# Two expert layers: the product back to the features in three rounded products

## What is computed

```python
x = _layernorm(x + _L0_attn_ref(x, Wqkv, Wout))          # causal attention, 16 heads of 8
x = _layernorm(x + _L0_ffn_ref(x, Wg, W1, W2, W3))       # 8 experts of 256, 2 per token
x = _layernorm(x + _L1_attn_ref(x, w_qkv, w_out, b_out)) # rotary positions, 16 heads of 8
x = _layernorm(x + _L1_ffn_ref(x, ...))                  # 4 experts of 512, 2 per token
```

## Time and profile before

| | |
|---|---|
| median of 3 runs | 2009.62 us (2008.22 to 2015.79) |
| the profiled execution | 2016.69 us, its span 2014.8 us |
| TensorE busy | 1766.9 us, 88% |
| VectorE | 1391.3 us, 69% |
| ScalarE | 1165.4 us, 58% |
| GpSimd | 96.9 us, 5% |
| first expert stage, first product back to last | 485.2 to 881.4 us |
| second expert stage, the same | 1696.7 to 2004.2 us |

### The profile page before, as it was taken

The page is one execution under the profiler, slowest core; times in us unless marked ns, Lnnn a source line. Parts: engine busy times, 40 slices in busy tenths (PEclk is TensorE's granted clock), DMA queues, the critical chain, the costliest instruction groups (busy, mean ns, idle before and its releaser), DMA issues.

```text
span 2014.8 us, 31350 instructions
## 1 busy us (share of the span) xinstructions
PE 1766.9 (88%) x9328; PEld 853.9 (42%) x9328; DVE 1391.3 (69%) x2540; ACT 1165.4 (58%) x1801; POOL 96.9 (5%) x123
## 2 busy tenths in 40 slices
PE   4558888886999999976999999999999986999897
PEld 2223333334655666632333333333333324554454
DVE  2257777775677777747788888898898834455544
ACT  2347777773444444420777777777777773444443
POOL 1000000000111001111000000000000000001100
PEclk8679999997999999985999999999999996999999
DMA  4441111101011010112000000010000001000000
GB/s 153 142 120 48 48 45 46 50 29 63 0 32 32 31 32 31 32 37 64 21 22 21 20 20 21 23 36 21 21 20 20 21 1 42 6 6 5 10 5 11
DMA packets 43323, 71.06 MB, mean 35 GB/s; under 512 B 13408, under 2 KB 22512, under 8 KB 42624
## 3 DMA queue, kind: packets, MB, share of 16 engines
q1 hardware_dynamic: 43264, 70.37, 10.8%
HBM read 44.14 MB, written 26.21 MB: 35 GB/s over the span
## 4 chain that ended last, share of the span: by engine, by line
PE 63%; DVE 9%; ACT 8%; DMA 7%; SPq 6%; issue 5%; POOL 1%; DVEq 0%; ACTq 0%; POOLq 0%
PE full_o L687 13%; PE score L674 11%; PE hid_pair L957 11%; PE bank L1057 9%; ACT probs L736 6%; DMA q_st<-q_scr 4%; PE max_pair L650 3%; PE causal_o L451 3%; SPq L614 2%; PE triple L435 2%; SPq L615 2%; PE bank L966 2%; DMA xs<-in_x 2%; PE bank L987 2%; DVE hid L1314 1%
## 5 line engine op out<-in xcount | busy, mean ns | idle before, releaser
L774 DVE TENSOR_REDUCE negmax<-max_pair 128x1 f32<-128x1024 f32 x512 | 599.9, 1218 | 69.4 <-PE max_pair L650 62.2
L736 ACT ACTIVATE probs<-score 128x512 f32<-128x512 f32 x1024 | 529.1, 604 | 150.7 <-PE score L674 150.7
L650 PE MATMUL max_pair<-k_st,q_st 64*128 64x512 f32 x1024 | 405.5, 474 | 22.4 <-DMA q_st<-q_scr 18.2
L674 PE MATMUL score<-q_st,k_st 64*128 64x512 f32 x1024 | 383.1, 451 | 33.4 <-ACT probs L736 24.4
L484 ACT ACTIVATE cprobs<-triple 128x1536 f32<-128x1536 f32 x192 | 271.3, 1451 | 95.9 <-PE triple L435 95.6
L674 PEld LDWEIGHTS score<-q_st,k_st 64*128 64x128 f32 x1024 | 170.7, 185 | 304.3 <-ACT probs L736 283.0
L687 PE MATMUL full_o<-probs,v_st 128*32 128x512 f32 x2048 | 273.1, 606 | 0.0
L650 PEld LDWEIGHTS max_pair<-k_st,q_st 64*128 64x128 f32 x1024 | 171.7, 191 | 80.3 <-DVE negmax L774 39.6
L957 PE MATMUL hid_pair<-x_hi,w_hi 128*128 128x512 f32 x384 | 205.6, 535 | 0.0
L435 PE MATMUL triple<-q_st,k_st 64*128 64x512 f32 (+3 forms) x768 | 146.8, 415 | 43.4 <-DMA q_st<-q_scr 36.8
L451 PE MATMUL causal_o<-cprobs,v_st 128*32 128x512 f32 (+3 forms) x1536 | 161.4, 517 | 21.2 <-DVE cprobs L514 17.6
(11 more groups left out here) (127 smaller groups left out, 1612.0 us busy)
## 6 DMA issues: line engine op xcount, KB each, us to landing
k_st<-k_scr SPq DMA_DIRECT2D x128, 64.0 KB
q_st<-q_scr SPq DMA_DIRECT2D x128, 64.0 KB
q_st<-q_scr SPq DMA_DIRECT2D x16, 512.0 KB
k_st<-k_scr SPq DMA_DIRECT2D x64, 104.0 KB
q_scr<-qk_hi SPq DMA_DIRECT2D x24, 256.0 KB, 2.9
k_scr<-qk_hi SPq DMA_DIRECT2D x24, 256.0 KB, 3.0
q_scr<-qk_lo SPq DMA_DIRECT2D x16, 256.0 KB, 2.9
k_scr<-qk_lo SPq DMA_DIRECT2D x16, 256.0 KB, 3.1
```

The source lines that it names most:

```text
L650: ins = nc.tensor.matmul(ring[slot][:, half, :], q_st[p][rows, qt * P:(qt + 1) * P], k_st[p][rows, j, half * CH:(half + 1) * CH], start=Tr ...
L674: nc.tensor.matmul(sbank[L.score_bank(e)][:, :], k_st[p][rows, j, kt * P:(kt + 1) * P], q_st[p][rows, q0:q0 + w], start=True, stop=True, t ...
L736: nc.scalar.activation(probs[s % NP][:, j, :], sbank[L.score_bank(e)][:, :], ACT.Exp, scale=SCALE).then_inc(L.exp_done, 1)
L774: nc.vector.tensor_reduce(negmax[:, qt // TPC, j, qt % TPC:qt % TPC + 1], ring[slot][:, :, :].rearrange("p a n -> p (a n)"), AXX, ALU.max, ...
```

## The change

The product back becomes three rounded products. Its weight (`w3`, `we2`) is split once a stage: `w2_hi` by ScalarE, the lower half by VectorE. Each block `hid` is split too: `hid_hi` by a rounding copy on ScalarE, one step behind the activation, `hid_lo` = `hid` - `hid_hi` by a subtraction on GpSimd. The product back waits for the lower half. `hid`, `hid_hi` and `hid_lo` have four buffers (`HB` = 4). The first products run three blocks ahead in both stages; in the first stage step 0 issues two of them and step 15 none. The banks (`h_banks`) stay as they are. GpSimd's work beside is now placed by step, behind the subtraction of its step. `we2` is loaded into the second weight's tile, and the four `rot` tiles share memory with halves of q and k.

```diff
@@ experts' tiles @@
-            hid = [osb(f"hid{i}", [P, CH]) for i in range(2)]
+            hid = [osb(f"hid{i}", [P, CH]) for i in range(HB)]
+            hid_hi = [osb(f"hid_hi{i}", [P, CH], F32R) for i in range(HB)]
+            hid_lo = [osb(f"hid_lo{i}", [P, CH], F32R) for i in range(HB)]
...
-        h_banks, h_lead = [2, 4], [1, 2]
+        h_banks, h_lead = [2, 4], [3, 3]
...
@@ pe_chunk @@
-                lead = n + h_lead[layer]
-                if lead < SPC:
-                    pe_hidden(pe, st, c, par, lead, layer)
-                elif front is not None:
-                    pe_hidden(pe, st, front, 1 - par, lead - SPC, layer)
+                for lead in pe_leads(n, layer):
+                    if lead < SPC:
+                        pe_hidden(pe, st, c, par, lead, layer)
+                    elif front is not None:
+                        pe_hidden(pe, st, front, 1 - par, lead - SPC, layer)
...
-                pe.wait_ge(st.hid_ready, c * SPC + n + 1)
-                nc.tensor.matmul(bank[0][:, :], w[:, n, :], hid[n % 2][:, :], start=(layer == 0 and n == 0),
-                                 stop=(n == SPC - 1)).then_inc(st.y_done, 1)
+                pe.wait_ge(st.hid_lower, c * SPC + n + 1)
+                w_up, w_low = w2_hi[:, n, :], (w3_lo if layer == 0 else we2_lo)[:, n, :]
+                for a, (w, x) in enumerate(((w_up, hid_hi), (w_low, hid_hi), (w_up, hid_lo))):
+                    last = nc.tensor.matmul(bank[0][:, :], w, x[n % HB][:, :],
+                                            start=(layer == 0 and n == 0 and a == 0), stop=(n == SPC - 1 and a == 2))
+                last.then_inc(st.y_done, 1)
+
+        def pe_leads(n, layer):
+
+            k = h_lead[layer]
+            if layer == 1:
+                return [n + k]
+            if n == SPC - 1:
+                return []
+            return [n + k] if n else [n + k - 1, n + k]
...
@@ act_chunk @@
+        def act_upper(act, st, c, n):
+
+            act.wait_ge(st.hid_ready, c * SPC + n + 1)
+            wait_used(act, st.y_done, c * SPC + n - HB + 1)
+            nc.scalar.activation(hid_hi[n % HB][:, :], hid[n % HB][:, :], ACT.Copy).then_inc(st.hid_upper, 1)
...
+                if n > 0:
+                    act_upper(act, st, c, n - 1)
                 act_beside(act, st, n, back, front, 1 - par, layer)
...
+            act_upper(act, st, c, SPC - 1)
             act.wait_ge(st.y_done, (c + 1) * SPC)
...
@@ act_end and dve_end, once a stage @@
+                    w2 = w3_raw if layer == 0 else we2_raw
+                    nc.scalar.activation(w2_hi[:, :, :], w2[:, :, :], ACT.Copy).then_inc(w2_upper, 1)
...
+                if n == plan[layer].norm + 1:
+                    dve.wait_ge(w2_upper, layer + 1)
+                    w2, low = (w3_raw, w3_lo) if layer == 0 else (we2_raw, we2_lo)
+                    nc.vector.tensor_tensor(low[:, :, :], w2[:, :, :],
+                                            w2_hi[:, :, :].bitcast(F32), ALU.subtract).then_inc(w2_lower, 1)
...
@@ dve_chunk @@
-                wait_used(dve, st.y_done, c * SPC + n - 1)
+                wait_used(dve, st.hid_lower, c * SPC + n - HB + 1)
...
@@ GpSimd @@
+        def pool_lower(pool, st, c, n):
+
+            pool.wait_ge(st.hid_upper, c * SPC + n + 1)
+            wait_used(pool, st.y_done, c * SPC + n - HB + 1)
+            nc.gpsimd.tensor_tensor(hid_lo[n % HB][:, :], hid[n % HB][:, :], hid_hi[n % HB][:, :].bitcast(F32),
+                                    ALU.subtract).then_inc(st.hid_lower, 1)
...
+            if back is not None:
+                if n == pl.norm2 - 1 - (layer == 0):
+                    bc.at(back)
+                    pool_rstd(pool, bc, st.stats2, st.rstd2, 1, back + 1)
+                for a, at in enumerate((pl.q, pl.k)):
+                    if n == at:
+                        pool.wait_ge(st.rot_done, 2 * back + a + 1)
+                        nc.gpsimd.tensor_tensor(rot[2 * a][:, :], rot[2 * a][:, :], rot[2 * a + 1][:, :],
+                                                ALU.add).then_inc(st.rot_sum, 1)
+            if front is not None and n == pl.norm - 1:
+                fc.at(front)
+                pool_rstd(pool, fc, st.stats, st.rstd, 0, front + 1)
...
+            for n in range(SPC):
+                pool_lower(pool, st, c, n)
+                pool_beside(pool, st, n, back, front, layer)
```

More of the change, by code:

```diff
@@ L38 @@
 CP = 6
+HB = 4
 PAIRS = KT * HG
@@ L280, in build_program @@
         with ExitStack() as overlay:
-            w_raw = [osb(f"w_raw{k}", [P, NH * P]) for k in range(2)]
+            with ExitStack() as raw_only:
+                w_raw = [raw_only.enter_context(nc.sbuf_tensor(f"w_raw{k}", [P, NH * P], F32)) for k in range(2)]
+            w_lo = [osb(f"w_lo{k}", [P, NH * P], F32R) for k in range(2)]
             w_hi = [osb(f"w_hi{k}", [P, NH * P], F32R) for k in range(2)]
-            w_lo = [osb(f"w_lo{k}", [P, NH * P], F32R) for k in range(2)]
+            we2_raw, we2_lo = (w[1][:, :].rearrange("p (n c) -> p n c", c=P) for w in (w_raw, w_lo))
+            w2_hi = osb("w2_hi", [P, NH, P], F32R)
             x_out = osb("x_out", [P, TPC, D])
@@ L301, in build_program @@
             qk_lo = [osb(f"qk_lo{i}", [P, CH]) for i in range(4)]
+            rot = [qk_hi[2], qk_hi[3], qk_lo[2], qk_lo[3]]
             expert_raw = osb("expert_raw", [2 * E0, E0, P])
@@ L955, in pe_hidden @@
             for k in range(2 if layer == 0 else 1):
-                for a, (w, x) in enumerate(((w_hi[k], x_hi[par]), (w_lo[k], x_hi[par]), (w_hi[k], x_lo[par]))):
-                    last = nc.tensor.matmul(hbank[2 * k + n % h_banks[layer]], w[:, slice_of(n)], x[:, :], start=(a == 0),
+                w_up, w_low = w_hi[k][:, slice_of(n)], w_lo[k][:, slice_of(n)]
+                for a, (w, x) in enumerate(((w_up, x_hi[par]), (w_low, x_hi[par]), (w_up, x_lo[par]))):
+                    last = nc.tensor.matmul(hbank[2 * k + n % h_banks[layer]], w, x[:, :], start=(a == 0),
                                             stop=(a == 2))
@@ L1040, in pe_chunk @@
             per = SPC // n_exp[layer]
-            w = w3 if layer == 0 else we2
             for n in range(SPC):
@@ L1065, in pe_end @@
             pe.wait_ge(w_lower, 2 if layer == 0 else 3)
-            if layer == 1:
-                pe.wait_ge(we2_loaded, 16)
-            for n in range(h_lead[layer]):
+            pe.wait_ge(w2_lower, layer + 1)
+            for n in range(h_lead[layer] - (layer == 0)):
                 pe_hidden(pe, st, 0, 0, n, layer)
@@ L1309, in dve_chunk @@
                     dve.wait_ge(st.s_done, h_banks[layer] + c * SPC + n + 1)
-                    nc.vector.tensor_tensor(hid[n % 2][:, :], act_s[n % 2][:, :], lin_u[n % 2][:, :],
+                    nc.vector.tensor_tensor(hid[n % HB][:, :], act_s[n % 2][:, :], lin_u[n % 2][:, :],
                                             ALU.mult).then_inc(st.hid_ready, 1)
@@ L1346, in pool_rstd @@
             nc.gpsimd.tensor_tensor(rstd[:, k, :], rstd[:, k, :], mhalf[:, :], ALU.pow).then_inc(sig, 1)
-        def pool_back(pool, pc, st, c, layer):
-            pool_rstd(pool, pc, st.stats2, st.rstd2, 1, c + 1)
-            if layer == 0:
-                for a in range(2):
-                    pool.wait_ge(st.rot_done, 2 * c + a + 1)
-                    nc.gpsimd.tensor_tensor(rot[2 * a][:, :], rot[2 * a][:, :], rot[2 * a + 1][:, :],
-                                            ALU.add).then_inc(st.rot_sum, 1)
@@ L1356, in pool_end @@
-        def pool_end(pool, st, layer):
-            pc = Chain(pool, st.pool_chain)
-            for c in range(2):
-                pool_rstd(pool, pc, st.stats, st.rstd, 0, c + 1)
-            with pool.Fori(0, 2 * B - 2) as c:
-                pc.at(2 + 2 * c)
-                pool_back(pool, pc, st, c, layer)
-                pool_rstd(pool, pc, st.stats, st.rstd, 0, c + 3)
-            for c in (2 * B - 2, 2 * B - 1):
-                pc.at(2 + 2 * (2 * B - 2) + c - (2 * B - 2))
-                pool_back(pool, pc, st, c, layer)
+        def pool_lower(pool, st, c, n):
[3 more added lines that the diff above has]
+                                    ALU.subtract).then_inc(st.hid_lower, 1)
@@ new lines, in build_program, with pool_chunk @@
+        pool_front, pool_back = [None], [None]
+        def pool_chunk(pool, st, c, back, front, layer):
+            for n in range(SPC):
+                pool_lower(pool, st, c, n)
+                pool_beside(pool, st, n, back, front, layer)
+        def pool_end(pool, st, layer):
+            pool_front[0], pool_back[0] = Chain(pool, st.pool_chain), Chain(pool, st.pool_back_chain)
+            for n in range(SPC):
+                pool_beside(pool, st, n, None, 0, layer)
+            pool_chunk(pool, st, 0, None, 1, layer)
+            with pool.Fori(1, 2 * B - 1) as c:
+                pool_chunk(pool, st, c, c - 1, c + 1, layer)
+            pool_chunk(pool, st, 2 * B - 1, 2 * B - 2, None, layer)
```

(2 more changed lines are left out.)

26 lines of the change are left out of this document (18 added, 8 removed).

## The result

The changed kernel takes 2556.9 us (median of 4 runs, 2551.0 to 2560.2) against 2011.5: a ratio of 1.270, 95% interval 1.268 to 1.273, or 545 us more. The forecast was 2370, its range 2200 to 2470. The direction was right and the size was not.

A forecast was written before the change was run, and what follows sets the result against it. It took waits on same-step products, through ScalarE's order and the first stage's two banks, to bind: 2016.7 + 217 (first stage) + 140 (second) + 5 (weight splits) = 2379 us profiled, so 2370; range 2200 to 2470.

The forecast's parts named there:

- rival (d): Both expert stages: GpSimd binds by rate; at 31 us a chunk it is under both stages, no chance of its own.
- The first loop, ScalarE's order: Both stages: the product back waits on ScalarE work that needs products of the same step; a gate-row step 4.35 us.
- The second loop, two banks at a lead of three: First stage: block n+3 starts only after activation and `lin_u` of n+1 free a bank; steps up to 6.4 us.
- Rival (b): First stage: without the bank loop, near 63 us a chunk, 2230 in all; 20% together with other partial overlap.
- The steps of the first stage: Sixteen step times listed for a first-stage chunk, sum 80.6 us against 51.2 before; +217 us for the stage.
- The steps of the second stage: Sixteen step times listed for a second-stage chunk, sum 59.2 us against 40.4 before; +140 us for the stage.
- the clock stays near 1: TensorE in both stages: listed as a sign that the forecast is right; waits of 1.75 us leave it at 1.00.
- Rival (a): TensorE's granted clock falls for part of a stage; a third at half clock gives 2550, a tenth 2420; 12%.
- the upper bound: GpSimd's subtraction takes 1.96 us if it always waits for a `hid`, instead of 1.27; 100 us more.
- Products: Product back on TensorE: three rounded products take 0.70 us instead of 0.86 a block, 41 us less work.
- Both weights' split: Before each stage: a copy and a subtraction of 2048 columns for the product back's weight, +5 us for both.
- The subtraction's lower bound: The subtraction takes 0.68 us, as the same form does on VectorE, instead of 1.27; 85 us less.

The follow-up runs named there:

- e4: Changed kernel with ScalarE's upper half of block n moved ahead of the gate copy of n; 2430 us, ratio 1.209.
- e9: Changed kernel with first products one and two blocks ahead as before the change, and the product back done one block later; 2168 us, ratio 1.078.
- e3: Changed kernel with first products one and two blocks ahead as before the change, nothing left out; 2785 us, ratio 1.386.
- e2: Changed kernel without the halves of `hid`: all three products back read a rounded `hid`, first products three blocks ahead; 2241 us, ratio 1.114.
- e7: Changed kernel with first products two blocks ahead in the first stage, three in the second as before; 2392 us, ratio 1.189.
- e12: Changed kernel with first products done three times in nine second-stage steps that have a wait; 2510 us, ratio 1.248.
- e1: Changed kernel without the halves of `hid`: three products back read a rounded `hid`, first products one and two blocks ahead; 1987 us, ratio 0.989.
- e6: Changed kernel with the subtraction for the lower half on VectorE, behind `hid` of the next block; 2516 us, ratio 1.250.

## Why the prediction was right in kind and short in size

**Which resource binds.** Right. Neither ScalarE (51% busy) nor GpSimd (17%) is short of time; the new links cost as latency. GpSimd has no rate problem: rival (d) is out.

**The first loop, ScalarE's order.** Right. In the second stage nothing else holds TensorE for long. With the upper half moved ahead (e4) 127 us come off, and with the product back a step later at the same lead (e9 against e3) the chunk falls from 70.3 to 49.8.

**The second loop, two banks at a lead of three.** Right, and shown by e2 (+254 us with no halves at all) and e7. Rival (b), that only one loop binds, is out in the first stage.

**The steps of the first stage.** One middle chunk, steps 0 to 15 by the starts of the product back (the next ones repeat it within 0.15 us a step): 7.6, 5.7, 4.4, 5.9, 5.2, 6.6, 8.5, 8.2, 6.1, 6.4, 4.4, 6.7, 8.4, 3.0, 4.4, 4.0. Steps 1, 2, 9, 10, 14 and 15 have the clock at 1.00 and are within 0.25 us of the forecast; 4 and 5, at 0.93, are 0.2 and 0.5 over. Step 3 is 3.1 over: the normalisation above holds `lin_u`, and then its six first products run at half clock (763.22 to 765.92), which is 6 x 0.20 = 1.2 of the 3.1. Steps 0, 6, 7, 8, 11 and 12 have the clock between 0.50 and 0.77 and are together 11.5 over. Step 13, at 0.75, is 0.7 under, which hides as much of the miss. Steps 0, 6, 10 and 12 and the end of step 3 in the sums by stretch, of the kernel after (the clock is the third number from the end):

```profile
742.28:749.85 7.57, 7.08 (x17) 4.83 (x18) 1.98 (x3) 3.77 (x7) 2.37 (x2) 0.55 0.00 0
...
763.22:765.92 2.70, 2.70 (x6) 2.12 (x7) 1.18 (x2) 0.00 (x0) 0.00 (x0) 0.50 0.00 0
...
777.77:786.24 8.47, 6.82 (x16) 4.12 (x14) 2.58 (x4) 1.60 (x3) 2.57 (x2) 0.70 0.00 0
...
807.05:811.45 4.40, 2.94 (x12) 1.61 (x10) 1.76 (x4) 1.60 (x3) 1.34 (x1) 1.00 0.00 0
...
818.13:826.53 8.40, 6.41 (x20) 5.06 (x18) 4.68 (x22) 4.59 (x7) 1.27 (x1) 0.50 0.00 0
```

Step 0 is the plainest: it has 12 first products, each 0.43 instead of 0.23 apart at half clock, which is 12 x 0.20 = 2.4 us, and it is 2.5 over.

**The steps of the second stage.** Here the same step can be read at two clocks. In steps 1, 3, 7 and 9 TensorE has no wait to speak of. In the kernel after (chunk from 2215.67) they last 3.58, 2.73, 2.73 and 2.73 us at a clock of 0.50, in e12 (chunk from 2200.31) 1.94, 1.70, 1.49 and 1.70 at 1.00, step 7 at 0.92; the forecast had 1.9, 1.4, 1.4 and 1.4. Steps 1 and 9 of both, after first:

```profile
2221.48:2225.06 3.58, 3.58 (x11) 2.89 (x11) 1.01 (x3) 0.00 (x0) 1.18 (x1) 0.50 0.00 0
2255.51:2258.24 2.73, 2.73 (x6) 2.17 (x7) 0.50 (x1) 0.00 (x0) 1.63 (x1) 0.50 0.00 0
```

```profile
2205.43:2207.37 1.94, 1.94 (x11) 1.63 (x11) 0.50 (x1) 0.00 (x0) 1.19 (x1) 1.00 0.00 0
2234.53:2236.23 1.70, 1.65 (x7) 1.05 (x7) 0.49 (x1) 0.00 (x0) 1.64 (x1) 1.00 0.00 0
```

These four steps, whose work e12 leaves as it was, are 4.9 us a chunk shorter there. In the kernel after itself step 9 of the chunk before had the clock at 1.00 (2184.58 to 2186.28) and took 1.70. Its other steps with the clock at 1.00 come out close to the list too: step 2 6.53 (forecast 6.5), 4 and 5 together 7.58 (7.8), 8 4.92 (5.1), 10 6.95 (6.9), 14 4.51 (4.5), 15 4.03 (3.9); step 13 alone is far off, 2.56 for 1.4. So the list of the second stage was close to right as a list at full clock; steps 6, 11 and 12 of e12, at 0.68 to 0.79, leave that open for themselves.

**The step that failed: "the clock stays near 1".** This is the assumption behind both sums: every product in them is priced at full clock. It rested on the earlier trace rows, a wait of 1.75 us that left the clock at 1.00 in the earlier trace rows. That was one such wait in 40 us; the changed kernel has one in most steps, and its clock is at 0.80 and 0.71. Rival (a) put a third of the time at half clock and came to 2550; the time is 2557, and the mean of 0.80 and 0.71 means 40% and 58% of the time at the lower level. It had 12%. The price is best seen in the same list of instructions at two clocks. Middle chunks of e1:

```profile
573.20:821.28 248.08, 237.22 (x1021) 169.38 (x1021) 184.19 (x455) 107.31 (x176) 25.54 (x30) 1.00 0.10 32
1750.81:1947.89 197.08, 172.66 (x731) 119.19 (x730) 106.43 (x350) 94.29 (x150) 18.20 (x20) 0.97 0.02 7
```

The 1021 and 731 products of the window are busy 237.2 and 172.7 us here and 325.1 and 255.5 in the kernel after: 17.6 and 16.6 us a chunk more. The chunks are 14.9 and 11.7 longer than forecast. Not all of these products are on the path. So the low clock is large enough for all of it, e12 shows it for at least 7.9 of the 11.7 of the second stage, and for the first stage it is read from the steps and no run isolates it.

The Trainium skill, "TensorE: Matmul & The Clock Gate", Part 1, says that the full clock is what activity earns and the lower one the default, and it describes kernels in which waits throw it back again and again. By that rule rival (a) had to be expected with more than its 12%; the trace agrees, at 0.50 and 1.00 in turn.

**The meeting of GpSimd and VectorE.** Under-sized. The forecast had 0.97 against 0.69 and let the upper bound speak for the subtraction only. It is VectorE that is held: `hid` has a mean of 889 and 861 ns, against means of 707 and 688 before, so (0.889 - 0.707) x 16 = 2.9 and 2.8 us a chunk, the normalisation 1.7 more in the chunk above (3.08 us for four that take 0.341 each alone), while the subtraction has a mean of 1384 ns against the 1270 taken, 1.8 a chunk. How much of this lies on the path no run separates, since e6, which removes the meeting, also changes VectorE's order. By the steps above it is at most 1.9 of the first stage's 14.9 in step 3, the rest of whose 3.1 is the clock. The steps at low clock hold 11.5, but steps 11 and 12 have a long `hid` as well (1.53 and 1.66 us), so the two are not cleanly apart.

The Trainium skill, "GPSIMD Engine Reference", Key points, names two kinds of VectorE instruction that contend with GpSimd, those with two SBUF inputs and those in a two-port mode. The trace agrees for the first, `hid`, up to 1.78 us, and it has the normalisation too, which reads one tensor and two columns; whether that one runs in a two-port mode no run here shows.

**The terms.** Products: -24 (e1), not -41. Both weights' split: nothing that can be seen, not +5. First stage +319 for +217, second +223 for +140: 185 us too little. For the profiled execution the sum gave 2379 and 2558 was measured, 179 more: the 185 less the 5 for the split and 1 outside. The 187 between forecast and median has 8 us more, mainly because the forecast was scaled down by 0.35%.

**The subtraction's lower bound.** e6 is the case of the bound, -85 in the forecast, and gave -41. The order in which VectorE takes the subtraction changes with it, which the bound left out.

## What to carry to other kernels

Where a link is added between two products of one block, draw the order of every engine through one step and look for a wait whose releaser was issued in the same step: here such a loop cost its whole latency in each step that has it. In the second stage a lead of three instead of two did not open it (70.9 and 70.3 a chunk), while doing the dependent product one step later did (e9 against e3: 617 us in all). More lead also needs more banks: a lead of three on two banks cost 254 us. And where waits come once a step, price TensorE's work at the lower clock too before adding up: here that is at least two thirds of what the forecast of the second stage missed, and large enough for the whole of it in both.

## What the runs showed of the chip

- TensorE's clock fell with waits of a few us in most steps. No wait for the subtraction in the second stage is over 4.1 us, their mean is 2.1 to 2.4, and the mean clock there is 0.71; across one wait of 2.40 us it went from 1.00 (2207.64) to 0.50 (2210.68).
- Repeated, useless products in the waits made the changed kernel faster: 12.4 us of them a chunk took 7.9 us off (e12).
- A VectorE instruction beside a GpSimd subtraction of 128 x 512 is lengthened far more than the subtraction is: a normalisation of 341 ns took up to 1334, `hid` of 690 up to 1781, while the subtraction itself kept a median of 1282 ns.
